# Last normalisation's moments on ScalarE, right factors scaled on ScalarE, exponentials with the head innermost, in a product-key layer on one core

## The reference

```python
q = jnp.einsum('bnd,de->bne', x, w_q)            # then batch-normalised, cut into 2 x 8 heads of 128
sim = jnp.einsum('pbnhd,hkpd->pbnhk', q, keys)   # 32 similarities per side and head
sx, ix = jax.lax.top_k(sim[0], TOPK)             # 8 best of 32, left and right side
sy, iy = jax.lax.top_k(sim[1], TOPK)
all_scores = (sx[..., :, None] + sy[..., None, :]).reshape(b, n, H, TOPK * TOPK)
scores, pk = jax.lax.top_k(all_scores, TOPK)     # 8 best pairs of a head
h = jnp.einsum('bnd,bnhkd->bnhk', x, wd)         # wd: rows of down_embed of the chosen experts
h = jax.nn.softmax(scores, axis=-1) * gelu_new(h)
out = jnp.einsum('bnhk,bnhkd->bnd', h, wu)       # wu: rows of up_embed
x = _layernorm(x + out)                          # no gain, no offset
```

## Time and profile before

| | |
|---|---|
| median of 3 runs | 738.68 us (736.33 to 741.09) |
| profiled execution | 743.06 us, span of its instructions 741.3 us |
| busy: VectorE, GpSimd | 590.3 us (80%), 456.8 us (62%) |
| busy: TensorE, ScalarE | 547.0 us (74%), 350.8 us (47%) |
| granted TensorE clock, mean | 0.909 of full speed |

### The profile page before, as it was taken

How to read it: one execution, slowest core, us unless ns; L and a number is a source line. 1 busy time by engine, 2 the same in 40 slices (tenths; PEclk the granted TensorE clock), 3 DMA queues, 4 the chain that set the end, 5 groups by cost and what they waited for, 6 DMA issues and landing times.

```text
span 741.3 us, 42186 instructions
## 1 busy us (share of the span) xinstructions
PE 547.0 (74%) x17799; PEld 459.0 (62%) x17799; DVE 590.3 (80%) x1860; ACT 350.8 (47%) x549; POOL 456.8 (62%) x623
## 2 busy tenths in 40 slices
PE   0445978887999678877365788777887778877776
PEld 0344867776887446646344677666776677766665
DVE  5534766785888569998578888999999999999982
ACT  4333555564667334655314344455544455544540
POOL 7523434453463234646217778898888888889981
PEclk9978898997999889999566799999999999999997
DMA  6684485777571101000001213222232322223211
GB/s 217 189 232 114 126 235 131 172 229 205 152 182 33 44 1 29 16 28 0 4 6 39 64 47 70 69 70 52 62 71 64 71 52 62 71 64 71 67 46 38
DMA packets 45574, 64.79 MB, mean 87 GB/s; under 512 B 5712, under 2 KB 37712, under 8 KB 42960
## 3 DMA queue, kind: packets, MB, share of 16 engines
q1 hardware_dynamic: 45520, 64.04, 33.7%
HBM read 36.49 MB, written 8.65 MB: 61 GB/s over the span
## 4 chain that ended last, share of the span: by engine, by line
DVE 39%; PE 36%; issue 18%; POOL 3%; DMA 1%; DVEq 1%; ACT 1%; SPq 0%; POOLq 0%; ACTq 0%
PE ps L745 9%; DVE top L1312 6%; PE ps L760 6%; PE ps L909 5%; PE ps L725 5%; DVE prod L1367 4%; DVE tile_rows L1149 4%; DVE wq_sb L1343 4%; PE ps L735 3%; PE ps L888 3%; DVE best L1323 3%; DVE r_x L1352 2%; DVE stats L1129 2%; DVE hid L1358 2%; PE ps L771 2%
## 5 line engine op out<-in xcount | busy, mean ns | idle before, releaser
L909 PE MATMUL ps<-up_sb,prod 128*128 128x128 f32 x512 | 80.4, 320 | 48.1 <-DVE prod L1367 47.9
L930 ACT ACTIVATE arena<-ps 128x512 f32<-128x512 f32 x128 | 70.5, 595 | 94.9 <-PE ps L745 94.8
L909 PEld LDWEIGHTS ps<-up_sb,prod 128*128 128x128 f32 x512 | 74.1, 227 | 54.5 <-DVE prod L1367 54.5
L888 PE MATMUL ps<-arena,hid 128*32 128x32 f32 x8192 | 81.5, 200 | 22.2 <-issue 18.3
L888 PEld LDWEIGHTS ps<-arena,hid 128*32 128x32 f32 x8192 | 76.8, 113 | 27.2 <-issue 19.4
L1093 DVE TENSOR_REDUCE row_max<-ps 128x8 f32<-128x768 f32 x64 | 61.0, 953 | 28.2 <-PE ps L735 27.5
L660 POOL TENSOR_TENSOR wq_sb<-wq_sb,tile_rows 128x1024 f32<-128x1024 f32 x32 | 76.3, 2385 | 9.3 <-POOL tile_rows L656 8.5
L745 PE MATMUL ps<-ident,arena 128*128 128x128 f32 x512 | 75.0, 295 | 1.9 <-issue 1.6
L1039 ACT ACTIVATE out_tile<-ps,shift,rstd 128x128 f32<-128x128 f32 x32 | 14.6, 458 | 121.3 <-POOL shift L684 121.3
L897 PEld LDWEIGHTS ps<-xT,downT_sb 128*128 128x128 f32 x512 | 64.3, 197 | 12.0 <-issue 11.0
L745 PEld LDWEIGHTS ps<-ident,arena 128*128 128x128 f32 x512 | 66.3, 155 | 3.8 <-issue 1.3
(11 more groups left out here) (157 smaller groups left out, 1336.8 us busy)
## 6 DMA issues: line engine op xcount, KB each, us to landing
arena<-r_x SPq DMA_DIRECT2D x128, 128.0 KB, 2.4
early<-terms SPq DMA_DIRECT2D x16, 360.0 KB
xT<-terms SPq DMA_DIRECT2D x16, 360.0 KB
hid<-terms SPq DMA_DIRECT2D x16, 360.0 KB
prod<-terms SPq DMA_DIRECT2D x16, 360.0 KB
x_tile<-in_x_wrapped SPq DMA_DIRECT2D x32, 128.0 KB, 6.6
x<-in_x SPq DMA_DIRECT2D x8, 256.0 KB, 2.7
xT_tile<-xT SPq DMA_DIRECT2D x32, 64.0 KB, 1.9
```

The costliest lines, as they stand in the source:

```text
L888: mm = nc.tensor.matmul(slots[32 * g:32 * g + 32, k, c], leftT[p][:, r // 2, r % 2, :], blocks_of[p][:, :, r // 2, r % 2, GROUP * g:GROUP ...
L909: mm = nc.tensor.matmul(ps[:, 6 + p, 0:P], pairs[:, c // 2, c % 2], up_sb[:, c, :], start=False, stop=(c == EC - 1))
L930: return nc.scalar.activation(out_ap, in_ap, ACT.Copy)
```

## The change

- `last_moments` leaves VectorE. ScalarE sums instead: a copy scaled by -1/128 with an accumulated output gives minus the mean (`minus_mean4`), and a square with that as its bias gives the sum of squared deviations (`square4`). Both write their elements to `scratch`. GpSimd's `last_scale` first turns the sum into a variance plus epsilon, and then goes on as before, its last instruction a product instead of a product with a constant.
- The product of the right exponentials with `rz` leaves GpSimd. ScalarE's `scale_exps` does it in place with eight activations of 32 elements, one for each head, whose scale is a column of `rz`.
- `rel_exp` is laid out as side, key, head instead of side, head, key. The exponential writes with a step of 8 words; GpSimd's `scale_right` and `scale_left` read it in the order of their other operand.

```diff
-        rel_exp = [tile_rows[:, 2560 + 512 * p:3072 + 512 * p].rearrange("p (a k) -> p a k", a=PH) for p in range(2)]
+        rel_exp = [tile_rows[:, 2560 + 512 * p:3072 + 512 * p].rearrange("p (a k h) -> p a k h", a=2, h=PK_HEADS) for p in range(2)]
...
             def scale_right(t, p):
-                pool.wait_ge(rz_done, t + 1)
-                pool.wait_ge(relexp_done, t + 1)
-                hold(pool)
-                ey = rel_exp[p][:, PK_HEADS:PH, :]
-                nc.gpsimd.tensor_tensor(ey, ey, bcast(rz[p][:], 2, KEYS), ALU.mult).then_inc(scaled, 1)
                 pool.wait_ge(scaled, t + 1)
                 pool.wait_ge(masked, 2 * t + 1)
                 hold(pool)
-                nc.gpsimd.tensor_tensor(right[p], right[p], bcast(ey.rearrange("p h j -> p j h"), 3, TERMS), ALU.mult
+                nc.gpsimd.tensor_tensor(right[p], right[p], bcast(rel_exp[p][:, 1], 3, TERMS), ALU.mult
                                         ).then_inc(right_ready, 1)
...
-                ex = rel_exp[p][:, 0:PK_HEADS, :].rearrange("p h i -> p i h")
+                ex = rel_exp[p][:, 0]
...
             def last_scale(t):
-                pool.wait_ge(d_var, t + 1)
+                pool.wait_ge(d_square, t + 1)
+                hold(pool)
+                nc.gpsimd.tensor_scalar(var4[:], square4[:], 1.0 / P, EPS, ALU.mult, ALU.add).then_inc(rstd_step, 1)
+                pool.wait_ge(rstd_step, 2 * t + 1)
                 hold(pool)
                 nc.gpsimd.tensor_tensor(rstd4[:], var4[:], minus_half[:, 0:1], ALU.pow).then_inc(rstd_step, 1)
-                pool.wait_ge(rstd_step, t + 1)
-                hold(pool)
-                nc.gpsimd.tensor_scalar(shift4[:], mom4[:, 0:1], rstd4[:], -1.0, ALU.mult, ALU.mult).then_inc(d_rstd, 1)
+                pool.wait_ge(rstd_step, 2 * t + 2)
+                hold(pool)
+                nc.gpsimd.tensor_tensor(shift4[:], minus_mean4[:], rstd4[:], ALU.mult).then_inc(d_rstd, 1)
...
-                nc.scalar.activation(rel_exp[p].rearrange("p a k -> p (a k)"), ps[:, p, :], ACT.Exp
+                nc.scalar.activation(rel_exp[p].rearrange("p a k h -> p a h k"),
+                                     ps[:, p, :].rearrange("p (a h k) -> p a h k", a=2, h=PK_HEADS), ACT.Exp
                                      ).then_inc(relexp_done, 1)
+            def scale_exps(t, p):
+                a.wait_ge(relexp_done, t + 1)
+                a.wait_ge(rz_done, t + 1)
+                for h in range(PK_HEADS):
+                    ey = rel_exp[p][:, 1, :, h]
+                    last = nc.scalar.activation(ey, ey, ACT.Copy, scale=rz[p][:, h:h + 1])
+                last.then_inc(scaled, 1)
+            def last_moments(t, p):
+                a.wait_ge(up_done, t + 1)
+                nc.scalar.activation(scratch[:], ps[:, 6 + p, 0:P], ACT.Copy, scale=-1.0 / P, accum_out=minus_mean4[:]
+                                     ).then_inc(d_mean, 1)
+            def last_square(t, p):
+                a.wait_ge(d_mean, t + 1)
+                nc.scalar.activation(scratch[:], ps[:, 6 + p, 0:P], ACT.Square, bias=minus_mean4[:], accum_out=square4[:]
+                                     ).then_inc(d_square, 1)
```

More of the change, by code:

```diff
@@ L216, in attention_and_product_keys @@
         out_tile = two("out_tile", [P, P])
-        stats4 = sb("stats4", [P, 6])
-        mom4 = sb("mom4", [P, 2])
+        scratch = sb("scratch", [P, P])
+        minus_mean4 = sb("minus_mean4", [P, 1])
+        square4 = sb("square4", [P, 1])
         var4 = sb("var4", [P, 1])
@@ L317, in attention_and_product_keys @@
         up_done = sem("up_done")
-        d_step = sem("d_step")
-        d_var = sem("d_var")
+        d_mean = sem("d_mean")
+        d_square = sem("d_square")
         rstd_step = sem("rstd_step")
@@ L1050, in d_act @@
                         rel_exps(t + 1, o)
+                    if have(t - 2):
+                        last_moments(t - 2, p)
+                    if have(t + 1):
                         best_exps(t + 1, o)
+                    if have(t - 2):
+                        last_square(t - 2, p)
+                    if have(t + 1):
+                        scale_exps(t + 1, o)
                     if have(t - 2):
@@ L1284, in split_constants @@
                 cols = slice(Q_SPLIT[part].start * KEYS, Q_SPLIT[part].stop * KEYS)
-                c_rest = rel_exp[0].rearrange("p a k -> p (a k)")
+                c_rest = rel_exp[0].rearrange("p a k h -> p (a k h)")
                 v.wait_ge(c_row_done, part + 1)
@@ L1368, in gate @@
                                     act4[:, :, half], ALU.mult).then_inc(gated_done, 1)
-            def last_moments(t, p):
-                v.wait_ge(up_done, t + 1)
-                V.bn_stats(stats4[:], ps[:, 6 + p, 0:P]).then_inc(d_step, 1)
-                v.wait_ge(d_step, 2 * t + 1)
-                need(v, out_ready, t)
-                hold(v)
-                V.bn_aggr(mom4[:], stats4[:]).then_inc(d_step, 1)
-                v.wait_ge(d_step, 2 * t + 2)
-                V.tensor_scalar(var4[:], mom4[:, 1:2], EPS, None, ALU.add).then_inc(d_var, 1)
             v.wait_ge(x3_kept, NQ)
@@ L1386, in d_dve @@
                         top_keys(t + 1, o)
-                    if have(t - 2):
-                        last_moments(t - 2, p)
                     if have(t):
```

## The result

The changed kernel takes 737.4 us against 739.6 us before (medians of 20 executions each); the ratio of the two is 0.9935, with a 95% interval of 0.9906 to 0.9965. By that ratio it is 0.65% faster, 4.8 us, where 12.4 us and 726.3 were forecast. The ratio takes only the executions within 1.5% of the fastest one of the same kernel (12 of the changed kernel's 20, 18 of the 20 before), and over all 20 of each the medians lie only 2.2 us, 0.3%, apart. The time lies 0.4 us above the upper end of the range.

The account below looks back on a forecast made before the run. VectorE's unbroken 10.05 us per last-stage tile was taken as the bound, falling to 9.57. 26 x 0.48 = 12.5, plus 0.4 for other tiles, less 0.5 at the end: 12.4 us off 738.68, 726.3 us; range 716 to 737.

Parts of the forecast that it names:

- What bounds the tile: Last stage: VectorE's unbroken 10.05 us before; afterwards a VectorE-GpSimd loop through the limits, 9.57 us, gaining 0.48 a tile.
- four holds of 0.9 us: `top_keys` waiting for late similarities in four of 25 tiles, said to explain the mean of 10.25 us over 10.05.
- The moments: `last_moments` frees 0.77 us of VectorE per tile; on ScalarE each moment activation costs 0.35 to 0.9 us.
- GpSimd's sum: GpSimd's work per tile: 9.6 us without layout effects, including 0.4 for the added one-column step and its wait.
- The layout: GpSimd's `scale_right` and `scale_left` together save 0.5 us, between 0.95 saved and 0.95 lost; pays nothing by itself.
- the row L588: GpSimd row at 2.75 ns an element; its slower-case rival put the two products 0.95 us up, 752 us, chance 0.1.
- The scalings: Eight ScalarE scalings of the right exponentials take 2.1 us with the tail and stay hidden behind GpSimd's work.
- TensorE's slow `up_projection` keeps its hold: TensorE's slow tiles go on holding `top_keys` as before, since the way from the gate's end is unchanged.
- the count of 26 tiles that gain 0.48 each: Last stage, 26 tiles between 430 and 696 us each gain 0.48, 12.5 us in all.
- The end: At the kernel's very end the last moments lie on the path and cost 0.5 us more.
- partial loss: Rival: ScalarE or GpSimd takes part of the gain, leaving 0.1 to 0.25 us a tile, 734 us; chance 0.17.
- nothing to the end: Rival: something outside these loops, block transfers or TensorE, paces the tiles, so the end stays, 737 us; chance 0.05.

Follow-up runs that it names:

- e12: e5 with `classes` done for only half of the keys, so its output differs; undisturbed tile 9.40 to 9.45 us, ratio to the kernel before 0.981.
- e4: Kernel before with only the moments moved to ScalarE, layout and scaling as before; undisturbed tile mostly 10.3 to 10.8 us, ratio to before 1.014.
- e3: Kernel before with only the `rel_exp` layout changed, moments and scaling left where they were; undisturbed tile 9.99 to 10.14 us, ratio to before 0.998.
- e1: Changed kernel plus five short unread TensorE products per loop tile, after the residual's product; no slow tiles, ratio to the kernel before 0.985.
- e5: Changed kernel plus two long unread TensorE products (384 columns each) per loop tile, ahead of the residual's product; ratio to the kernel before 0.979.
- e10: Changed kernel plus one long unread TensorE product per loop tile, ahead of the residual's product; ratio to the kernel before 0.983, median 725.4 us.

## Why the prediction was wrong, point by point

- **What bounds the tile**: right for the undisturbed tile. VectorE's own work before, and the loop `top_keys`, candidates, `classes`, limits, `edges` after; 9.57 forecast, 9.55 measured, and e12 moved it to 9.42 by cutting only GpSimd's part of that loop. The prediction was wrong to take four holds of 0.9 us for the whole rest of the mean of 10.25: they give 0.14 of the 0.20. The other part lay in the loop's first three tiles, 32.1 us for three times 10.05, where the gate also waits for the outer products.
- **The moments**: right in the price on VectorE. On ScalarE the first takes 0.39 us with its accumulator read, inside the 0.35 to 0.9.
- **GpSimd's sum**: right, the added instruction with its wait costs 0.37 (600.03 to 600.40) for my 0.4. e4 shows that without the rest it would have been the bound.
- **The layout**: 0.77 us saved on the two products, between the 0.5 taken and the 0.95 of the favourable end; the range's other end, the row L588, did not apply. That it pays nothing by itself: e3. The trace thus goes part of the way with the rule of the Trainium skill, GPSIMD Engine Reference, "Performance pitfalls for Q7 kernels": the long step did cost, but 0.4 us for 768 elements where by its ratio it would be an estimated 0.6. The page's remedy speaks of the innermost step, and here the long one lies one dimension further out, behind an element that is repeated. What I had not priced is the other side of the same edit, 0.5 us for the exponential's stepped output; it fell where ScalarE had room.
- **The scalings**: 2.06 us for my 2.1, hidden as said.
- **The step that failed** is "TensorE's slow `up_projection` keeps its hold", and with it the count of 26 tiles that gain 0.48 each. The hold of one slow tile was read rightly, 1.1 us longer, but their number was taken over from the kernel before: 4 of 25, where the changed kernel has 9. Four tenths of the gain of the 25 tiles went there. e1, e5 and e10 held the clock with work that nobody needs, and the tile's gain came back. About a third more was missing in the loop's first three tiles, which I counted as gaining although VectorE does not set their pace; there the two profiles differ by no more than other kernels of this study do, so that part may be chance. Why the changed kernel loses the clock more often stays open.
- **The end**: the 0.5 us that I put on the last moments can't be seen; the ends of the profiled executions scatter by over 5 us.
- The rival of a "partial loss" had about the right size (734; 4.8 us off 738.7 are 733.9) and the wrong mechanism. The rival of "nothing to the end" had 737 and named TensorE among what might pace the tiles; I gave it 0.05 because VectorE has no idle time in an undisturbed tile, and did not ask how many tiles would be undisturbed. None of mine was about the clock. The granted clock stood in the earlier trace rows, and the slow tiles in the earlier trace rows; I used them only for the length of a hold.

## What to carry to other kernels

A tile's sum from the trace can be right to 0.02 us and the kernel still hardly move, when another engine's clock changes with the rhythm. If a few tiles of a steady stretch are slow because TensorE has half its clock after a wait, count them as a term of their own, and expect another number after any change of rhythm. Profile more than one execution of each kernel before counting, or look at the mean clock of all. Here one unneeded product of 0.75 us per tile, put where TensorE would wait, brought the changed kernel from 0.9935 to 0.983, while two of them in the kernel before changed nothing that could be seen. It has to be few instructions: with five short products the loop's first three tiles took 38.0 us, against 34.6 without and 31.8 with the single long one.

## What the runs showed of the hardware that was not expected

- ScalarE's exponential of 512 elements from PSUM took 598 ns when it wrote to neighbouring words and 1111 to 1123 ns when it wrote with a step of 8 words (changed kernel, e3).
- An activation with an accumulated output is followed by a separate instruction of 187 or 194 ns in the mean (the two moments) that reads the accumulator; from the start of the first moment to the start of `best_exps` are 0.29 us.
- GpSimd's product of 256 elements took 617 ns while its second operand changed with every 32nd element, and 728 ns when it changed with each (e3).
- After its outer products and an idle time of 1.3 to 2.3 us, TensorE's granted clock fell to 0.5 in some tiles and not in others of the same rhythm. In the changed kernel it fell after 1.35 to 1.39 us and not after 1.74 to 1.76. With 0.8 to 1.1 us of idle time left and a long product ahead, it fell in none of the loop's tiles (e10).
- Five or seven short products more on TensorE made the first three tiles in the loop longer, 38.0 and 39.3 us against 31.8 (e10) to 34.9 (e3) in all the other kernels, with an idle time of 3.06 us in e1 that no row of an engine ends. Instruction transfers of 16 KB run in this stretch, and none from 475 us to the loop's end.
- The start of the product-key stage differed between executions with the same code ahead of it, 380.8 to 390.8 us for the first `top_keys` over the profiles of this study; a difference of spans of that size says nothing about a change in a later stage.
